# Moving VectorE units, the last half of a group norm and one copy to other places of a sequence loop, and transposes ahead of value sums

## The reference

```python
xn = layernorm(x)
# recurrent branch, 16 heads of 16 x 16 state
r, k, v, g = ((xn + dx * lora_p(lerp)) @ W_p.T for p in "rkvg")
w = exp(-exp(lora_d(xn + dx * lora_d(lerp))))
state = w[t][..., None] * state + k[t] v[t]            # scanned over the tokens of a sequence
y[t] = r[t] (state_before + u * k[t] v[t])
s = (silu(g) * group_norm(y)) @ oW.T                   # norm over the 16 channels of a head
# gate branch
z = xn + attention(rmsnorm(xn))                        # 16 heads, causal, rotary, low-rank keys and values
gate = z + moe(rmsnorm(z))                             # top 2 of 8 experts and one shared
out = x + s * silu(gate)
```

## Time and profile before

| | us |
|---|---|
| median of 3 runs | 2274.21 |
| lowest, highest | 2270.74, 2276.09 |
| the profiled execution | 2276.78 |
| its span | 2275.0 |
| one sequence of phase_c (start of one lora stretch to the next) | 209 to 212 |

### The profile page before, as it was taken

How to read it: one execution, slowest core, us unless ns; L and a number is a source line. 1 busy time by engine, 2 the same in 40 slices (tenths; PEclk the granted TensorE clock), 3 DMA queues, 4 the chain that set the end, 5 groups by cost and what they waited for, 6 DMA issues and landing times.

```text
span 2275.0 us, 37286 instructions
## 1 busy us (share of the span) xinstructions
PE 2062.7 (91%) x11722; PEld 1243.2 (55%) x11723; DVE 1794.2 (79%) x2906; ACT 974.1 (43%) x2556; POOL 846.5 (37%) x666
## 2 busy tenths in 40 slices
PE   7998599997988999998999889998989998899887
PEld 4554599997445445544554455455445544554554
DVE  5997466664697889779897988898798879887985
ACT  3444244442274237334623652373347235612741
POOL 1335200001543364336435542643364346326430
PEclk9999799998999999999999999999999999999998
DMA  6554411113222022211211230222122112302210
GB/s 174 145 158 138 146 54 54 52 55 116 64 57 80 1 65 71 61 37 47 66 47 47 61 86 4 61 66 70 29 56 66 47 47 57 79 15 60 61 48 10
DMA packets 145727, 151.18 MB, mean 66 GB/s; under 512 B 47664, under 2 KB 105648, under 8 KB 145584
## 3 DMA queue, kind: packets, MB, share of 16 engines
q1 hardware_dynamic: 138288, 136.73, 22.0%
q0 software_dynamic: 3072, 8.41, 1.1%
q10 hardware_dynamic: 4224, 4.19, 0.6%
HBM read 121.71 MB, written 27.43 MB: 66 GB/s over the span
## 4 chain that ended last, share of the span: by engine, by line
issue 24%; PE 23%; DVE 18%; POOL 8%; ACT 2%; DMA 0%; POOLq 0%; DVEq 0%; ACTq 0%
PE bank L1375 8%; PE bank L1238 4%; DVE arena L1777 4%; POOL arena L2064 3%; PE bank L1292 3%; DVE arena L1797 3%; DVE arena L1790 3%; PE bank L1255 3%; PE bank L1388 2%; POOL arena L2058 2%; DVE arena L2011 1%; ACT arena L1587 1%; POOL arena L2079 1%; PE bank L1265 1%; DVE arena L1852 1%
## 5 line engine op out<-in xcount | busy, mean ns | idle before, releaser
L2058 POOL TENSOR_TENSOR arena<-arena 128x512 f32<-128x512 f32 x256 | 337.1, 1319 | 567.9 <-DVE arena L1797 491.5
L1375 PE MATMUL bank<-arena 128*128 128x512 f32 (+2 forms) x1312 | 438.6, 489 | 6.8 <-DVE arena L1927 6.8
L1171 PE MATMUL bank<-arena 128*128 128x512 f32 (+2 forms) x768 | 360.5, 614 | 6.8 <-ACT arena L1542 5.4
L1797 DVE TENSOR_TENSOR_SCAN arena<-arena 128x512 f32<-128x512 f32 x256 | 361.9, 1414 | 1.7
L1587 ACT ACTIVATE arena<-bank,arena 128x128 f32<-128x128 f32 (+3 forms) x512 | 266.3, 531 | 194.9 <-DVE arena L1777 193.8
L1375 PEld LDWEIGHTS bank<-arena 128*128 128x128 f32 x1312 | 249.9, 203 | 177.2 <-issue 142.1
L1790 DVE TENSOR_TENSOR arena<-arena 128x512 f32<-128x512 f32 x256 | 249.0, 973 | 40.6 <-DMA arena<-values 36.5
L1238 PE MATMUL bank<-arena 64*128 64x128 f32 (+3 forms) x1024 | 207.5, 481 | 71.4 <-ACT arena L1587 49.7
L1171 PEld LDWEIGHTS bank<-arena 128*128 128x128 f32 (+2 forms) x768 | 139.5, 190 | 198.7 <-issue 171.5
L1777 DVE TENSOR_REDUCE arena<-bank 128x2 f32<-128x256 f32 (+3 forms) x256 | 206.9, 808 | 39.0 <-PE bank L1241 39.0
L1596 ACT ACTIVATE arena<-bank 128x128 f32<-128x128 f32 (+3 forms) x512 | 196.4, 441 | 72.3 <-PE bank L1255 72.3
(11 more groups left out here) (200 smaller groups left out, 2960.8 us busy)
## 6 DMA issues: line engine op xcount, KB each, us to landing
arena<-values SPq DMA_DIRECT2D x256, 256.0 KB, 3.4
arena<-in_L_attn_h SPq DMA_DIRECT2D x16, 512.0 KB, 10.4
arena<-in_W1T SPq DMA_DIRECT2D x8, 1024.0 KB
arena<-in_W2T SPq DMA_DIRECT2D x8, 1024.0 KB
sorted_rows<-arena SPq DMA_DIRECT2D x42, 128.5 KB, 9.9
arena<-sorted_rows SPq DMA_DIRECT2D x40, 128.5 KB, 2.1
arena<-in_b2row SPq DMA_DIRECT2D x40, 128.0 KB, 2.9
gate_rows<-arena SPq DMA_DIRECT2D x39, 128.0 KB, 1.7
```

Of the source, the lines that this page charges most:

```text
L1171: last = nc.tensor.matmul(dst[rows, :], w, x, start=(n == 0), stop=(n == len(pairs) - 1))
L1375: last = nc.tensor.matmul(dst[o], w, x, start=first, stop=last_one)
L1797: nc.vector.tensor_tensor_scan(state[n % STATES][:, 1:T + 1], proj["w"][:, m, :], kv[n % 2], VEC["init"][:, m * HD + j:m * HD + j + 1], AL ...
L2058: nc.gpsimd.tensor_tensor(prods[(n + 2) % PRODS], state[n % STATES][:, 0:T], proj["r"][:, m, :], ALU.mult).then_inc(prod_done, 1)
```

## The change

Constants: EARLY 24 to 22, STEPPED 22 to 20, AHEAD 4 to 2, so two units are ahead of attention, units 2 to 19 in its steps, 20 to 22 in the norm and 23 to 31 in experts. lat goes to the end of QKV, its copy on ScalarE into attention's step 1. In experts, read_out(1) goes from turn 5 to turn 8 of VectorE behind ln_gate(0), the reciprocal and scale of half 0 one turn later each, and mean_last to the end of TensorE's experts. center_last, the square and var_last go to the start of the next sequence. The reductions of groups 4 to 7 move. In a step of attention turn_probs stands ahead of weigh_values.

```diff
-EARLY = 24
-STEPPED = 22
-AHEAD = 4
+EARLY = 22
+STEPPED = 20
+AHEAD = 2
-QKV = "sp0 sp1 lat q2 q3 q4 q5 q6 q7".split()
+QKV = "sp0 sp1 q2 q3 q4 q5 q6 q7 lat".split()
-PRE_BANKS = ([6, 7, 3, 5, 0, 1, 2] + 5 * [3, 5, 6, 7, 0, 1, 2])[:len(PRE)]
+PRE_BANKS = ([6, 7, 3, 5, 0, 1, 2] + 5 * [3, 5, 6, 7, 0, 1, 2])[:len(PRE) - 7] + [0, 1, 2, 3, 5, 6, 7]
...
 # TensorE, before_attention
                 lora_pair(b, "v", "k", th[0])
+                if ended is not None:
+                    var_last(ended)
                 lora_a("d", 4, 1)
...
 # TensorE, attention, the loop over steps
-                    if i == PSTEPS:
-                        reduce_state(b, STEPPED // 4 - 1)
+                    if i < PSTEPS + 1:
+                        turn_probs(b, i - LAG)
                     done = i - LAG - 1
                     if done >= 0 and done % GSTEPS >= NT:
                         weigh_values(b, done // GSTEPS, done % NT)
-                    if i < PSTEPS + 1:
-                        turn_probs(b, i - LAG)
...
 # TensorE, behind the loop
                 spread_inverse(b, GROUPS - 1)
-                for i in range(1, NT):
-                    wo(i, early)
+                wo(1, early)
+                reduce_state(b, STEPPED // 4 - 1)
                 pe.wait_ge(y_out, GROUPS * b + GROUPS)
                 wo(0, [GROUPS - 1])
                 wo(1, [GROUPS - 1]).then_inc(made2, 2)
+                wo(2, early)
+                wo(3, early)
...
 # TensorE, experts
-                    if half:
-                        reduce_state(b, STEPPED // 4)
...
-                    if e == 2:
-                        reduce_state(b, EARLY // 4)
-                    elif e == 6:
-                        reduce_state(b, EARLY // 4 + 1)
-                    elif e == ME:
-                        mean_last(b)
+                    for at, g in ((2, 5), (4, 6), (ME, 7)):
+                        if e == at:
+                            reduce_state(b, g)
                     if e:
                         down(e - 1)
-                var_last(b)
+                mean_last(b)
...
 # ScalarE: the copy of lat leaves before_attention and stands in attention
+                    if i == LAG - 1:
+                        act.wait_ge(made, pre.made(b, "lat"))
...
 # VectorE, before_attention
+                if ended is not None:
+                    center_last(ended)
                 for name in ("v0", "k0", "v1", "k1", "d0", "d1"):
                     blend(name)
...
-                outer(b, 3)
                 if ended is not None:
                     gate_rows(ended, 1)
                     residual(ended)
-                scan(b, 2)
                 for name in QKV:
-                    if name == "q2":
-                        unit(b, AHEAD - 1)
...
 # VectorE, between(e) in experts
-                    if e < 4:
+                    if e < 6:
                         unit(b, EARLY + 4 + e)
-                    elif e == 5:
-                        read_out(b, 1)
+                    elif e == 6:
                         ln_inv(b, 0)
-                    elif e == 6:
+                    elif e == 7:
                         ln_scale(b, 0)
-                    elif e == 7:
-                        center_last(b)
                     elif e == 8:
                         ln_gate(b, 0)
+                        read_out(b, 1)
...
 # GpSimd: products 2 and 3 leave before_attention, rstd stands ahead of product 30,
 # the square of half 1 at the start of before_attention
```

More of the change, by code:

```diff
@@ L1137, in sequence @@
                         store_sequence(b - 1)
-                    if n == EARLY + COPIES and not last:
+                    if n == 28 and not last:
                         sp.wait_ge(pv_mm, CHUNKS * b + 2 * CHUNKS)
@@ L1491, in _ @@
             experts(B - 1, True)
+            var_last(B - 1)
             gates(B - 1, 0)
@@ L1576, in before_attention @@
                 nc.scalar.activation(x2, s_in, ACT.Copy).then_inc(x2_kept, 1)
-                act.wait_ge(made, pre.made(b, "lat"))
-                nc.scalar.activation(lat_tok.rearrange("p t c -> p (t c)"), bank[pre.bank("lat")][:, 0:NT * ND], ACT.Copy).then_inc(a_read, 1)
             def attention(b):
@@ L1620, in attention @@
                         exp(2 * i + 1)
+                    if i == LAG - 1:
+                        act.wait_ge(made, pre.made(b, "lat"))
+                        nc.scalar.activation(lat_tok.rearrange("p t c -> p (t c)"), bank[pre.bank("lat")][:, 0:NT * ND],
+                                             ACT.Copy).then_inc(a_read, 1)
                 act.wait_ge(pv_mm, CHUNKS * b + 2 * CHUNKS)
@@ L2021, in _ @@
             experts(B - 1, True)
+            center_last(B - 1)
             ln_inv(B - 1, 1)
@@ L2042, in gather, with head_rstd, head_rms @@
                                          in_offset=bass.IndirectOffsetOnAxis(ap=idx[:, i:i + 1], axis=0)).then_inc(g_loaded, 16)
-            def head(b):
+            def head_rstd(b):
                 g.wait_ge(var_done, b + 1)
                 nc.gpsimd.tensor_tensor(rstd, var_eps, neg_half, ALU.pow).then_inc(rstd_done, 1)
+            def head_rms(b):
                 g.wait_ge(ms_done, b + 1)
@@ L2058, in product, with before_attention @@
                 nc.gpsimd.tensor_tensor(prods[(n + 2) % PRODS], state[n % STATES][:, 0:T], proj["r"][:, m, :], ALU.mult).then_inc(prod_done, 1)
-            def before_attention(b):
+            def before_attention(b, ended):
+                if ended is not None:
+                    square_last(ended)
                 for n, x in enumerate(MIX_ORDER):
@@ L2069, in before_attention @@
                         product(b, 1)
-                    elif n == 3:
-                        product(b, 2)
-                        product(b, 3)
                     name, rows = ("ckv", P) if n == 0 else (f"q{n - 1}", P)
@@ L2111, in experts, with square_last @@
                 for n in range(EARLY + 3, UNITS):
+                    if n == UNITS - 2 and not final:
+                        head_rstd(b + 1)
                     product(b, n)
                 if not final:
-                    head(b + 1)
+                    head_rms(b + 1)
+            def square_last(b):
                 g.wait_ge(last_read, 4 * b + 1 + 1)
@@ L2118, in _ @@
             gather(0)
-            head(0)
+            head_rstd(0)
+            head_rms(0)
             g.wait_ge(weights_in, 16 * NW)
-            before_attention(0)
+            before_attention(0, None)
             attention(0)
@@ L2124, in _ @@
                 experts(b, False)
-                before_attention(b + 1)
+                before_attention(b + 1, b)
                 attention(b + 1)
             experts(B - 1, True)
+            square_last(B - 1)
             g.wait_ge(g_loaded, 64 * B)
```

## The result

| | before | after |
|---|---|---|
| median of 5 runs, us | 2272.12 | 2285.63 |
| lowest, highest | 2270.74, 2276.09 | 2283.36, 2286.19 |
| span of the profiled execution | 2275.0 | 2284.3 |
| mean granted clock | 0.963 | 0.950 |

The ratio is 1.0054, interval 1.0040 to 1.0069: slower by some 12 us (13.5 by the medians). The forecast was +6.8 us and a median of 2281, range 2255 to 2302. Sign and range held. Two steps of the sum did not: some 30 us of gain that was counted on did not come, and 19 us came from a step taken at nothing. That these errors cancel in good part is luck, so the agreement says less than it seems to.

A forecast was written before the change was run, and what follows sets the result against it. TensorE, busy 91% of the span, was taken as the bound, with VectorE nearly full in attention. Meetings with clock +39.9, end +4.5, relief -24 and attention -13.6 gave +6.8 us: median 2281 us, range 2255 to 2302.

The forecast's parts named there:

- units, reductions, lat moved: Ahead of and in attention: relief of 3.0 us and 1.7 us from moved reductions, in each of eight sequences.
- the signs that I had named: TensorE waits 6 us on read_out, L1852 waits under 1.5, attention 1 to 2 shorter, half clock at meetings, L1977 waits less.
- The meeting: Where two sequences meet: first product 4.1 us later behind read_out, variance matmul 0.86; 5.0 us per meeting, bounds 4.5 to 5.5.
- The clock at the meeting: Where two sequences meet: the clock falls each time and a little longer, 0.7 us more per meeting.
- rival B: Where sequences meet: the clock's fall costs 3.9 us each instead of 0.7, +22 us, 2303; chance 0.15.
- Relief ahead of attention: Ahead of attention: scans and outers leave VectorE's queue, lat fills the remaining wait; 3.0 us less per sequence, bounds 2.0 to 3.9.
- Attention: In attention's steps: moved state reductions and smaller terms save 1.7 us per sequence, bounds 0 to 3.5.
- Turning ahead of the value sums is taken at nothing: In attention's steps: transposes ahead of value sums change nothing, bounds 0.5 us either way.
- Rival D: In attention: the transposes' place pays, a third of TensorE's 6.2 us waits on exponentials goes; 16 us, 2265; chance 0.10.
- The end: Behind the last sequence: mean, centre, square, variance and root follow the final additions one by one; +4.5 us, bounds 3.5 to 6.
- Experts' units at nothing: In the experts: two more units, 3.9 us on VectorE, fit into 7.7 us of its idle time without holding TensorE.
- rival C: Whole kernel: meetings lose what the two reliefs give, gains near 5.5 us per sequence; 2275, no change; chance 0.13.

The follow-up runs named there:

- e_norm: The kernel before with only the group norm at a sequence's end moved as in the change; 2312.41 us, ratio 1.0177.
- e_weigh: The changed kernel with the value sums again ahead of the transposes in attention; 2303.97 us, ratio 1.0138.
- e_read7: The changed kernel with read_out(1) moved to the front of turn 7 on VectorE, ahead of ln_scale and the lerp; 2252.91 us, ratio 0.9922.
- e_best: e_read7 with four unused filling matmuls between the halves of the norm's transposes; 2229.11 us, ratio 0.9814.
- e_lat: The changed kernel with lat put back ahead of q2 and its ScalarE copy back in its old place; 2295.22 us, ratio 1.0110.
- e_turn: The kernel before with only the transposes put ahead of the value sums in attention; 2257.90 us, ratio 0.9945.
- e_afill: e_fill with four unused filling matmuls added between the halves of the norm's transposes; 2251.74 us, ratio 0.9919.
- e_bfill: e_turn with one and two filling matmuls ahead of the halves of the norm's transposes and two ahead of var_last; 2249.55 us, ratio 0.9911.
- e_fill: The changed kernel with five unused matmuls between the last down product and mean_last; 2257.93 us, ratio 0.9943.
- e_pad3: The changed kernel with three extra 0.86 us matmuls per sequence, in turns 3, 4 and 5 of the experts; 2304.17 us, ratio 1.0137.
- e_pad1: The changed kernel with one extra 0.86 us matmul per sequence, in turn 4 of the experts; 2294.94 us, ratio 1.0104.

## Why the forecast came out, and where it was wrong

Adding the parts one by one, as differences to the kernel before, and beside them my terms:

| step | forecast | measured |
|---|---|---|
| group norm moved (e_norm) | 7 x 5.7 + 4.5 = +44.4 | +41.1 |
| units, reductions, lat moved (e_norm to e_weigh) | -8 x 4.7 = -37.6 | -8.1 |
| transposes ahead (e_weigh to the change) | 0 | -19.5 |
| sum | +6.8 | +13.5 |

For a sequence that another follows my terms add up to 5.7 - 3.0 - 1.7 = +1.0 us, and +1.0 was measured; the table shows that this is not because the terms were right. The steps that failed are the second and the third. All the signs that I had named came out (the wait on read_out, rotations below 1.5 us, attention 1 to 2 us shorter, half clock at every meeting, L1977's wait from 4.6 to 2.9 us), the one on attention for a reason that I had taken at nothing.

**The meeting: right.** The first product starts 3.85 us later behind the last down product (4.1 forecast), TensorE waits 5.14 us on read_out, and the variance matmul (1.13) is added. e_read7 takes the wait away and gets 32 us back.

**The clock at the meeting: right, and what follows behind the norm left out.** Over ten microseconds the granted clock is 0.83 once and 0.66 six times, where it was 0.83 five times and 1.00 twice. That is 0.34 x 10 x 2 = 6.8 us at 1.2 GHz for most, 6.3 on average, against 2.4 before. But 2.5 of the 6.8 pass while TensorE still waits for read_out. What the fall takes is seen in the matmuls: 0.95 us in the matmul of the mean and 1.22 in the first products, 2.2 in all, against an average of 1.2 before, so 1.0 us more, where I took 0.7 and rival B 3.9. What I left out is the norm. Behind it the half clock lasts 10.2 us in all eight sequences of the changed kernel, and in the kernel before only in five (granted 0.70 over 17 us); in the other three it lasts 3.4 (0.90). The kernel before, in a sequence with the short fall:

```profile
1564.70:1623.50 58.80, 55.68 (x190) 31.12 (x189) 52.71 (x100) 12.98 (x28) 19.55 (x16) 0.97 0.09 25
```

With the long one the experts' stretch is 61.2 to 61.5 us, as in the row above from 1352.70. So the 6.8 us between them cost 2.6. In e_best the first 3.4 cost nothing; if that holds here too, the long fall costs some 2.6 us and not the 5.1 that I took for it. The Trainium skill ("TensorE: Matmul & The Clock Gate", "What's actually happening") says for modelling that the warm-up costs under 1% of a typical span. It speaks there of the start of a kernel; here the falls come back in every sequence, and filling one idle stretch per sequence gives 1.2%.

**Relief ahead of attention: right, and a little low.** In the first sequence, which has neither a meeting nor a variance matmul, the stretch went from 54.4 to 50.2 us: 4.2, beyond my bound of 3.9. The changed kernel:

```profile
570.80:621.00 50.20, 49.16 (x126) 20.29 (x126) 26.86 (x45) 14.37 (x25) 26.45 (x22) 0.95 0.19 48
```

The six later ones give 2.4 in the mean, since the variance matmul and the fall at the meeting now lie in them. e_lat assigns about 1.2 us of the relief to lat.

**Attention: near in total, wrong in cause; this is a step that failed.** I took 1.7 us from moved reductions and nothing from "Turning ahead of the value sums is taken at nothing". The stretch did get 1.0 us shorter in the mean, but e_turn alone gives all of it (77.3 to 76.3), and e_weigh, with every reduction moved and the old order, keeps the kernel before's 77.5 in the first sequence (both at a granted clock of 1.00). So the moved reductions are worth nothing there, and 13.6 us of the forecast gain were not to be had. The last reduction left step 32, and in its place TensorE waits:

```profile
1331.59 0.85 PE L1255 MATMUL bank<-arena 128*128 128x128 f32 x6 [1.72 <-ACT arena L1591]
```

A matmul that stands in another engine's shadow isn't time to be won. Rival D, at 0.10, had the right place, ScalarE's wait for the transposes, and its 16 us are a fair size (13 and 19). It was wrong on where the gain would show: TensorE's waits on the exponentials, a third of which it wanted to go, rose. My reason against it, that VectorE is last in those steps, overlooked that VectorE's wait for scores runs back over exponentials and copies on ScalarE to those transposes; that chain is read from the waits above.

**What became of the relief.** From e_norm to e_weigh the stretch ahead of attention is 3.1 us shorter, and yet a steady sequence takes 215.0 us in both. The experts' stretch gives back 2.1 us (63.4 to 65.5), attention and norm 1.0. e_norm:

```profile
1363.40:1426.80 63.40, 56.94 (x186) 32.99 (x187) 53.26 (x103) 14.15 (x29) 17.52 (x15) 0.91 0.09 26
```

and e_weigh:

```profile
1573.70:1639.30 65.60, 59.62 (x196) 33.55 (x196) 56.56 (x107) 14.03 (x29) 21.79 (x17) 0.89 0.16 44
```

The clock in it is lower: that accounts for up to 0.02 x 65 = 1.3 us of the 2.1, another reduction (1.0) for much of the rest. That the relief comes back once the falls are filled is what e_afill beside e_bfill shows. Which idle time sets off the long fall behind the norm stays open. The norm's wait is one of 3.3 us here, where the kernel before has two of at most 1.8, and e_best, which differs from e_read7 only by the filling there, has 3.4 us of half clock or none behind the norm where e_read7 has 10.2. But e_fill, which differs from the changed kernel only at the meeting, has 6.8 there in place of 10.2, so it isn't the norm's wait alone.

**The end: +7.5, not +4.5.** The chain from the last additions to the root's reciprocal grew by 5.0 us (from 3.1 to 8.1), as I had it within half a microsecond; two of its matmuls run at half clock:

```profile
2258.64 2.08 PE L1303 MATMUL bank<-arena 128*128 128x512 f32 x2 [2.49 <-DVE arena L1806]
...
2262.62 2.08 PE L1307 MATMUL bank<-arena 128*128 128x512 f32 x2 [1.90 <-POOL arena L2117]
```

The other 2.5 us lie in the experts ahead of it. **Experts' units at nothing:** e_best's stretch there is 58.8 us, as long as the kernel before's at the same granted clock of 0.97, with a reduction more in it, so the cover held. **Balance (rival C)** is how the moved parts stand with idle time filled; it did not hold in the change as made.

## What to carry to other kernels

Where TensorE is the bound and waits in every turn of a loop, price the clock's fall behind the wait together with the wait. Take the price from two turns of the same loop with and without the fall: here 3.4 us at half clock cost 1.6 us ahead of attention (53.8 and 52.2 in e_best) and nothing behind the norm. Then try two cheap remedies: put the operation waited for ahead of what doesn't need to be first, and fill the idle time with matmuls into a bank that is free. When asking what an order on one engine is worth, follow the waits of every engine behind it: the wait in which the gain showed was not that of the engine that was reordered. A forecast that comes true as a sum should still be taken apart, part by part.

## What the runs showed of the hardware that was not expected

Sequences settle into a repeated length, with the clock falling at the same places: 211.7 us for five sequences running in the changed kernel, 208.2 in both e_turn and e_fill, 215.0 in e_norm, e_weigh and e_pad3, though their work per sequence differs. In one execution a small edit can therefore come out as zero: in e_pad1's profiled one, six sequences take 1272.8 us against 1272.6 in the changed kernel, with 5.2 us of matmuls more in them and less half clock, while the median over its executions rose by 9. What ties the lengths to each other wasn't tried.

VectorE's lerp takes 1.42 us for two instructions in the changed kernel and 2.07 in the earlier trace rows. There GpSimd's square runs beside the first of the two, which takes 1.41 us; the second, with nothing beside it, takes 0.74. In the changed kernel GpSimd does nothing then, and both take 0.75. With the outer and scan of the earlier trace rows that is the third operation of VectorE that takes half as long again or more. Over the trace of the kernel before, all 48 outers with no GpSimd instruction beside them take 0.68 to 0.69 us and all 176 such scans 1.27 to 1.29; the 24 outers with GpSimd beside them throughout take 1.47 to 1.69.
